# Pairwise Strassen K and V: the attention sum first in each batch, and one product of the first K half moved behind the odd batch's scores

## The reference

```python
x = x + xattn(layernorm(x), ctx)      # q = x Wq + bq ; k, v = split(ctx Wkv + bkv); rotary on q and k
                                      # 16 heads of 32: softmax(q k^T * 64**-0.5, mask) v, then Wo, bo
x = x + attn(layernorm(x))            # causal self attention, 16 heads
x = x + ffn(layernorm(x))             # 8 experts, the 2 best by the gate, softmax of their logits
```

## Time and profile before

| | |
|---|---|
| median of 3 runs | 830.67 us (829.15 to 832.28) |
| the profiled execution | 831.04 us, of it the span of instructions 829.2 us |
| mean granted TensorE clock | 0.961 |
| TensorE, matmuls | 760.4 us busy, 92% |
| VectorE | 574.8 us busy, 69% |
| ScalarE | 408.2 us busy, 49% |
| GpSimd | 340.0 us busy, 41% |

### The profile page before, as it was taken

The page is one execution under the profiler, slowest core; times in us unless marked ns, Lnnn a source line. Parts: engine busy times, 40 slices in busy tenths (PEclk is TensorE's granted clock), DMA queues, the critical chain, the costliest instruction groups (busy, mean ns, idle before and its releaser), DMA issues. The chain is left out here.

```text
span 829.2 us, 23209 instructions
## 1 busy us (share of the span) xinstructions
PE 760.4 (92%) x9494; PEld 660.5 (80%) x9495; DVE 574.8 (69%) x1293; ACT 408.2 (49%) x930; POOL 340.0 (41%) x364
## 2 busy tenths in 40 slices
PE   8999979979997997999899799798889999789997
PEld 7998869878896986888798688787667777668884
DVE  6766876975876686597577668746679998932236
ACT  5435646553563554555455464535447666213330
POOL 1654445454443644436354354522123222036740
PEclk9999999998999998999899999999999999969999
DMA  8211201111011010110101011013483234834548
GB/s 289 112 53 40 73 5 49 60 64 53 16 47 52 9 53 1 54 59 2 53 8 54 19 35 60 2 52 120 145 349 154 115 140 174 319 123 165 189 140 304
DMA packets 23317, 78.99 MB, mean 95 GB/s; under 512 B 3344, under 2 KB 4752, under 8 KB 20144
## 3 DMA queue, kind: packets, MB, share of 16 engines
q1 hardware_dynamic: 19536, 65.50, 21.7%
q0 software_dynamic: 3680, 12.06, 4.3%
HBM read 58.93 MB, written 18.61 MB: 94 GB/s over the span
## 5 line engine op out<-in xcount | busy, mean ns | idle before, releaser
L167 PE MATMUL quad<-wparts,othi 128*128 128x512 f32 (+1 forms) x104 | 49.2, 473 | 33.1 <-DVE otlo L1019 33.1
L501 POOL TENSOR_TENSOR wraw<-craw 128x516 f32<-128x516 f32 x14 | 18.6, 1326 | 135.9 <-issue 131.0
L1356 PE MATMUL bank<-ctx_parts_hi,wparts 128*128 128x258 f32 x224 | 68.7, 307 | 0.8 <-DVE ctx_parts_lo L890 0.7
L890 DVE TENSOR_TENSOR ctx_parts_lo<-craw,ctx_parts_hi 128x1032 fp32r<-128x1032 f32 (+1 forms) x56 | 64.8, 1158 | 2.6 <-ACT ctx_parts_hi L626 2.6
L1381 PE MATMUL bank<-wparts,ctx_parts_hi 128*128 128x256 f32 x224 | 64.6, 288 | 0.3 <-DVE kb_even L962 0.3
L1357 PE MATMUL bank<-ctx_parts_hi,wparts 128*128 128x258 f32 x224 | 63.5, 283 | 0.0
L1358 PE MATMUL bank<-ctx_parts_lo,wparts 128*128 128x258 f32 x224 | 63.4, 283 | 0.0
L1383 PE MATMUL bank<-wparts,ctx_parts_hi 128*128 128x256 f32 x224 | 63.0, 281 | 0.0
L1384 PE MATMUL bank<-wparts,ctx_parts_lo 128*128 128x256 f32 x224 | 62.8, 280 | 0.0
L626 ACT ACTIVATE ctx_parts_hi<-craw 128x1032 fp32r<-128x1032 f32 (+1 forms) x56 | 47.2, 843 | 26.9 <-POOL craw L509 26.6
L661 ACT ACTIVATE wraw<-wraw,nmax 128x257 f32<-128x257 f32 x96 | 47.9, 501 | 23.9 <-DVE nmax L983 23.9
(11 more groups left out here) (413 smaller groups left out, 2719.4 us busy)
## 6 DMA issues: line engine op xcount, KB each, us to landing
craw<-ctx_t_dram SPq DMA_DIRECT2D x32, 516.0 KB, 4.3
expert_lo<-weights_dram SPq DMA_DIRECT2D x8, 1024.0 KB, 12.2
expert_hi_scratch<-wraw SPq DMA_DIRECT2D x16, 512.0 KB, 2.6
wparts<-expert_hi_scratch SPq DMA_DIRECT2D x8, 1024.0 KB, 8.6
wraw<-weights_dram SPq DMA_DIRECT2D x6, 1024.0 KB, 4.9
expert_lo<-ffn_out_scratch SPq DMA_DIRECT2D x16, 256.0 KB, 5.2
x<-x_dram SPq DMA_DIRECT2D x8, 256.0 KB, 4.5
craw<-weights_dram SPq DMA_DIRECT2D x2, 1024.0 KB, 4.9
```

The lines of the kernel that those rows point to most:

```text
L167: pe.matmul(psum, ahi(c), bhi(c), start=(c == 0), stop=False)
L890: dve.tensor_tensor(dst[1], src, dst[0].bitcast(F32), ALU.subtract).then_inc(s_clo, 1)
L1356: pe.matmul(psum, whi_i[:, i, cols], hi[:, i, :], start=own and i == 0, stop=False, skip_group_check=not own)
```

## The change

It alters the order of the work and nothing of what is computed. On VectorE `o_sum(b - 1)` becomes the first work of each even and odd batch, `v_sum(p, S_11)` goes ahead of the masks of an even batch, and `o_lo` comes right behind the masks (even) or behind `pair_parts` (odd). ScalarE and GpSimd get `o_hi` and `o_bias` earlier to match; GpSimd does `diagonals` ahead of the context sums in an odd batch and behind them in an even one. TensorE does product (0, 6) of a pair behind the scores of the odd batch, where it stood at the end of the even one; ScalarE's `k_copy(q, 0, 6)` moves behind `exp(b, 0)` of the odd batch. In the odd batch the extra step, the spread diagonals and `attend` go ahead of (1, 7), and V's product 5 goes ahead of its product 2, so that `v_copy(p, 5)` moves into the odd batch. (1, 1) and (1, 3) change places, and the mask of the next batch is made later. In batch 3 `PLAIN - 1` is written as `PAIR_FIRST * 2 - 1`, the same number.

```diff
--- before.py
+++ after.py
@@ -306,10 +306,10 @@
             L_HI, L_LO, L_PRODUCT, L_COPY, L_SUM = range(1, 6)
 
 
-            K_PRODUCTS = ((0, 2), (0, 5), (0, 1), (0, 6), (0, 3), (0, 7), (1, 2), (1, 5), (0, 4), (1, 3), (1, 1), (1, 6),
+            K_PRODUCTS = ((0, 2), (0, 5), (0, 1), (0, 6), (0, 3), (0, 7), (1, 2), (1, 5), (0, 4), (1, 1), (1, 3), (1, 6),
                           (1, 7), (1, 4))
             K_COPIES = ((0, 5), (0, 1), (0, 6), (1, 5), (0, 4), (1, 1), (1, 6), (1, 4))
-            V_PRODUCTS = (2, 5, 1, 6, 3, 7, 4)
+            V_PRODUCTS = (5, 2, 1, 6, 3, 7, 4)
             V_COPIES = (5, 1, 6, 4)
 
             def k_product_of(q, c, k):
@@ -570,24 +570,24 @@
                         if b == PLAIN - 2:
                             ctx_sums_late(q)
                     elif b % 2 == 1:
+                        o_bias(b - 1)
+                        diagonals(b)
+                        if b < B - 1:
+                            k_sin(b + 1, 0)
                         if q <= PAIR_LAST:
                             ctx_sums_early(q)
-                        o_bias(b - 1)
-                        if b < B - 1:
-                            k_sin(b + 1, 0)
-                        diagonals(b)
                         if b < B - 1:
                             k_sin(b + 1, 1)
                         ln_and_bias(t, j)
                         if b < B - 1:
                             k_sin(b + 1, 2)
                     else:
+                        o_bias(b - 1)
                         for i in range(3):
                             k_sin(b + 1, i)
-                        o_bias(b - 1)
-                        diagonals(b)
                         if q <= PAIR_LAST:
                             ctx_sums_late(q)
+                        diagonals(b)
                         ln_and_bias(t, j)
                 ln_pool(pool, TILES + 1)
                 o_bias(B - 1)
@@ -784,16 +784,15 @@
                         k_copy(q, 0, 5)
                         part_hi(q, O_T4)
                         k_copy(q, 0, 1)
-                        k_copy(q, 0, 6)
 
                 def even_step(b, t, j):
                     p, q = b // 2, b // 2 + 1
                     more = q <= PAIR_LAST
                     last = t == TILES - 1
-                    v_copy(p, 5)
                     v_copy(p, 1)
                     if more:
                         part_hi(q, O_X1)
+                    before_o_hi(b)
                     exp(b, 0)
                     exp(b, 1)
                     v_copy(p, 6)
@@ -805,42 +804,42 @@
                     for g in range(G):
                         pt_evac(b, g)
                     v_copy(p, 4)
-                    before_o_hi(b)
                     if more:
                         part_hi(q, O_T32)
                         k_copy(q, 0, 5)
+                        k_copy(q, 0, 1)
                         part_hi(q, O_T4)
-                        k_copy(q, 0, 1)
                     if j == 0:
                         ln_apply(t + 1, x[:, 0 if last else t + 1, :])
-                    if more:
-                        k_copy(q, 0, 6)
-                    else:
+                    if not more:
                         w_hi(AK)
 
                 def odd_step(b, t, j):
                     p, q = (b + 1) // 2, (b + 3) // 2
                     last = t == TILES - 1
-                    for g in range(G):
+                    exp(b, 0)
+                    k_copy(p, 0, 6)
+                    for g in range(1, G):
                         exp(b, g)
                     k_copy(p, 1, 5)
+                    before_o_hi(b)
+                    k_copy(p, 0, 4)
                     pt_evac(b, 0)
                     pt_evac(b, 1)
-                    k_copy(p, 0, 4)
+                    k_copy(p, 1, 1)
                     pt_evac(b, 2)
                     pt_evac(b, 3)
-                    k_copy(p, 1, 1)
-                    next_mask(b)
-                    before_o_hi(b)
+                    k_copy(p, 1, 6)
                     if j == 1:
                         xt_hi(t + 1)
-                    k_copy(p, 1, 6)
                     if j == 3:
                         qt_evac(t + 1)
+                    next_mask(b)
                     if q <= PAIR_LAST:
                         part_hi(q, O_T1)
+                    v_copy(p, 5)
                     k_copy(p, 1, 4)
-                    if b == PLAIN - 1:
+                    if b == PAIR_FIRST * 2 - 1:
                         w_hi(WO)
                     if last:
                         act.wait_ge(s_qmm, TILES)
@@ -1136,13 +1135,14 @@
                     p, q = b // 2, b // 2 + 1
                     more = q <= PAIR_LAST
                     last = t == TILES - 1
+                    o_sum(b - 1)
+                    v_sum(p, S_11)
                     begin_step(b, j)
-                    v_sum(p, S_11)
+                    o_lo(b - 1, (b - 1) % BT)
                     if more:
                         part_lo(q, O_X1)
                     v_sum(p, S_12)
                     v_sum(p, S_22)
-                    o_sum(b - 1)
                     inverse_sums(b)
                     pair_parts(b)
                     if more:
@@ -1153,7 +1153,6 @@
                         if t == 2:
                             dve.wait_ge(s_x, 16 * (TILES - 1))
                         ln_stats(t + 1, x[:, 0 if last else t + 1, :])
-                    o_lo(b - 1, (b - 1) % BT)
                     if more:
                         part_lo(q, O_T32)
                     if j == 0:
@@ -1171,21 +1170,21 @@
                 def odd_step(b, t, j):
                     p, q = (b + 1) // 2, (b + 3) // 2
                     last = t == TILES - 1
+                    o_sum(b - 1)
                     begin_step(b, j)
                     k_sum(p, 0, S_12)
                     k_sum(p, 0, S_22)
                     if j == 3:
                         q_rotate(t + 1)
-                    o_sum(b - 1)
                     inverse_sums(b)
                     pair_parts(b)
+                    o_lo(b - 1, (b - 1) % BT)
                     k_cos(b + 1, 0)
                     k_sum(p, 1, S_11)
                     k_cos(b + 1, 1)
-                    o_lo(b - 1, (b - 1) % BT)
+                    k_sum(p, 1, S_12)
                     if j == 1:
                         xt_lo(t + 1)
-                    k_sum(p, 1, S_12)
                     k_sum(p, 1, S_22)
                     if q <= PAIR_LAST:
                         part_lo(q, O_T1)
@@ -1530,8 +1529,6 @@
                         k_product(PAIR_FIRST, 0, 1)
                     diagonals_spread(b)
                     attend(b, j)
-                    if b == PLAIN - 2:
-                        k_product(PAIR_FIRST, 0, 6)
 
                 def even_step(b, t, j):
                     p, q = b // 2, b // 2 + 1
@@ -1552,27 +1549,26 @@
                         k_product(q, 0, 1)
                     diagonals_spread(b)
                     attend(b, j)
-                    if more:
-                        k_product(q, 0, 6)
 
                 def odd_step(b, t, j):
                     p = (b + 1) // 2
+                    k_product(p, 0, 6)
                     k_product(p, 0, 3)
                     k_product(p, 0, 7)
                     k_product(p, 1, 2)
                     k_product(p, 1, 5)
+                    k_product(p, 0, 4)
                     probs_transposed(b)
-                    k_product(p, 0, 4)
+                    k_product(p, 1, 1)
                     k_product(p, 1, 3)
-                    k_product(p, 1, 1)
+                    k_product(p, 1, 6)
                     extra_step(b, t, j)
-                    k_product(p, 1, 6)
-                    v_product(p, 2)
+                    diagonals_spread(b)
+                    attend(b, j)
                     k_product(p, 1, 7)
                     v_product(p, 5)
                     k_product(p, 1, 4)
-                    diagonals_spread(b)
-                    attend(b, j)
+                    v_product(p, 2)
                     v_product(p, 1)
 
                 def last_step(b, j):
```

## The result

| | before | after |
|---|---|---|
| median | 830.71 us (829.15 to 832.28) | 785.83 us (784.58 to 787.63) |
| profiled execution, its span | 831.04, 829.2 us | 784.58, 782.8 us |
| mean granted TensorE clock | 0.961 | 0.984 |

The ratio is 0.946, with a 95% interval of 0.944 to 0.949 over four runs of each. The forecast was 792.0 (778 to 805): faster as said, and by 6 us more.

A forecast was written before the change was run, and what follows sets the result against it. TensorE sets the pace, its idle time is the gain, and VectorE's late masks limit it: seven pairs at 32.3 and six at 32.5 us save 39.7, batch 3 costs 1.0, giving 792.0 us (778 to 805).

The forecast's parts named there:

- The 45 us: Output product in seven even batches: the waits for `otlo` and the half clock behind them go, 45 us in all.
- The new wait: Ahead of (0,7) in the odd batch: TensorE waits 1.1 us for mask, exp and ScalarE's copy of the bank.
- a hole in VectorE's late stretch that waits for ScalarE: VectorE from `v_sum(S_22)` to the first odd mask: listed as a sign that the forecast is wrong; no size given.
- the 2.23 us of the earlier trace: Three `k_cos` at the stage's end: taken as their time alone, against 4.00 us beside the context sums.
- So 0.2 less: Pairs of a tile's batches 0 and 1: statistics (1.01 us) stand in for `q_trig` (1.21), so 32.3 us a pair.
- the 0.35 us of contention: VectorE's part `O_T32`: the later diagonals now fall on it, +0.35 us, estimated between 0 and 0.46.
- I leave the other small holes in: TensorE from (0,7) to the next even scores: only one hole of 0.27 us goes, 14.37 becoming 14.1 us.
- the zero for the swap of (1,1) and (1,3): TensorE's reordered products: each finds its sum or copy a product earlier; zero, bounded by 0.3 us either way.
- The little that may be lost lie ahead of the new wait and are covered by it: GpSimd's later diagonals, there by +13.2 us where TensorE wants them at about +13.1: no cost to the pair.
- VectorE doesn't bind: Rival: milder contention, mask in time, no wait ahead of (0,7); 52 us gained, 778 us; chance 0.18.
- The clock falls: Rival: wait ahead of (0,7) grows to 2.7 us, half clock costs 1.67 more; 43 us lost, 835 us; chance 0.03.
- Below 1.94 us the trace shows no fall, so it is decided there: TensorE's clock behind a wait: 1.94 us left it at 1.00, 4.73 us brought it to 0.62.

The follow-up runs named there:

- e3: The kernel before with the attention sum moved alone (GpSimd's diagonals as in the changed kernel, TensorE's product order kept); 779.78 us.
- e5: The changed kernel with GpSimd's diagonals back ahead of the late context sums in even batches; 790.14 us.
- e8: The changed kernel with GpSimd's two late context sums done on only 32 of 258 columns; 782.16 us.
- e1: The changed kernel with product (0,6) and its copy back at the end of the even batch; 779.28 us.
- e7: The changed kernel with the copy of (0,6) behind all four exps of the odd batch; 815.17 us.

## Why the prediction was right, and where it was off

**The 45 us were right.** All seven waits for `otlo` are gone, the clock in the stage is 1.00, and e3 shows that this part alone does it.

**The new wait was right in mechanism.** In the pair 2/3: mask +16.99 (forecast +16.91), (0,7) at +18.56 (+18.4), wait 0.80 us instead of 1.1 (0.96 if counted from the start that the forecast counted from, since TensorE was ready at +17.60, not at +17.29), and none where "issue" had taken it. The pair came out at 32.45 us on average against 32.5. But the sum that led there was right by luck, through two errors of opposite sign. It kept `k_cos` at 4.00 us, and it is 3.58, as the diagonals no longer lie beside its first part (e5, where they do: 3.98). And it said that VectorE would have no hole from `v_sum(S_22)` to the mask; it has one of 0.36, because the copy of (0,1) comes from TensorE, which hadn't become faster there. e8 shows that this is the binding link: with 2.2 us more slack on VectorE the mask doesn't move. The signpost "a hole in VectorE's late stretch that waits for ScalarE" was named as a sign against the forecast, and it is one. The second half of the pair was lucky too: (0,7) starts 0.16 us later than forecast, and the rest of the pair takes 13.87 us instead of 14.1.

The forecast also misread `k_cos`: it took the 2.23 us of the earlier trace rows for its time alone. GpSimd does its diagonals beside it there, in the kernel before:

```profile
570.20 0.62 POOL L533 TENSOR_TENSOR pdiag_hi<-p_last_and_rinv_hi,const 128x256 fp32r<-128x256 f32 x1
570.77 1.07 POOL L536 TENSOR_TENSOR pdiag_lo<-p_last_and_rinv_lo,const 128x256 fp32r<-128x256 f32 x1
```

With the sums on 32 columns (e8) it is 1.62. The sum didn't use this figure, but what VectorE pays for the sharing is larger than the forecast took it to be.

**The pair 0/1 is nearly the whole error of the sum.** Forecast 32.3, measured 31.29 on average (30.81 typically). 7 x 1.01 is 7.1 us of the 7.4 by which the stage (413.73) is under the forecast (421.1). Two terms of its sum were mis-sized:
- The mask was to stand at +16.7 and stands at +15.80; (0,7) starts at +17.37 instead of +18.2, with no wait listed. The forecast took the list of the pair 2/3 and exchanged two durations ("So 0.2 less"). It should have asked what GpSimd does beside each of them, and where in the list each stands. In the pair 0/1 the diagonals fall on the layernorm statistics, not on `O_T32`: the 0.35 us of contention in the sum are absent (1.22 against 1.64), `k_cos` is 0.42 shorter, and the inverse sums take 0.55 instead of 0.71 (237.44 to 237.99). There is no hole: the statistics stand ahead of `k_sum`, so the list reaches it at +14.01 (244.84), when the copy of (0,1) has ended, at +13.76. And from there to the mask it is 1.79 us, where the pair 2/3, with `q_trig` behind `k_sum`, has 3.12.
- From (0,7) to the next even scores the forecast had 14.1, 14.37 less one hole of 0.27. It is 13.44 here (261.64 - 248.20) and 13.87 in the pair 2/3. "I leave the other small holes in" was the step that failed, and with it the zero for the swap of (1,1) and (1,3). In the batch that was measured there was a second hole, 0.13 us ahead of V's product 5 (275.00 after 274.75), and a third ahead of (1,6), which waited for the copy of (1,1), the product right before it in the old order. Behind the four transposes of the extra step the next matmul, (1,6), came 0.74 us after their start; now it is the diagonals' matmul, after 0.36. First the kernel before, then the changed one:

```profile
270.81 0.60 PE L1233 MATMUL quad<-const,xn 128*128 128x128 f32 x4
271.55 0.39 PE L1356 MATMUL bank<-ctx_parts_hi,w_sums_hi 128*128 128x258 f32 x1
```

```profile
254.30 0.60 PE L1232 MATMUL quad<-const,xn 128*128 128x128 f32 x4
254.66 0.36 PE L1432 MATMUL quad<-pdiag_hi,same_head 128*128 128x256 f32 x1
```

In e3, which keeps the old order of products, it is 0.74 still. 0.27 + 0.13 + 0.38 is 0.78 of the 0.93 us; each broken place also cost 0.10 us on the matmul behind the break (last section), which about fills the rest.

**Against that, two costs weren't in the sum.** The even attention of the pair 2/3 waits 0.19 us for the diagonals, which run beside `O_T32`. e5, with the diagonals early, has its scores at +14.12 where the changed kernel has +14.59, so the late diagonals cost TensorE 0.47 us there; this doesn't show in the time, since (0,7) waits for the mask anyway. And the waits on "issue" (0.18, 1.06 and 0.96 us) fall into three pairs that are 0.3, 0.2 and 1.5 us longer than their like; the middle one only took the place of the wait ahead of (0,7). With the first pair, 32.41 us, which waits 1.10 us for a copy of V and 0.28 for the residual sum, they are why the pairs 0/1 are 31.29 on average and 30.81 typically. The forecast's "The little that may be lost lie ahead of the new wait and are covered by it" held in the pair 2/3.

**Small terms.** Batch 4 began 1.18 us later (forecast +1.0). The diagonals did take their cost from `O_22` (1.06 before, 332.84 - 332.23 = 0.61 after) to `O_T32`. The Trainium skill (GPSIMD Engine Reference, its table of specifications) speaks of VectorE operations with two SBUF inputs; the trace agrees here, since `BATCH_NORM_STATS2`, with one input, takes 0.68 us beside the diagonals (242.10) and 0.68 without them. Held against both kinds of pair ahead of the run, it would have pointed to the pair 0/1 as the one without that cost.

**The rivals.** "VectorE doesn't bind" (778) is the time of the kernel without the moved (0,6), e1 and e3. To go by the busiest engine, as this rival does, misses the wait in the changed kernel: there VectorE is busy 77% of the pair 2/3 and still sets it, through an order. "The clock falls" (835) is real in mechanism: the fall came after waits of 2.3 us (e7) and, outside the stage, of 1.74 (e1), less than the 2.7 in the forecast's case, and costs 1.46 us a time instead of 1.67 (e7). "Below 1.94 us the trace shows no fall, so it is decided there" doesn't hold across these runs. Behind its waits of 0.8 us the changed kernel's clock stayed at 1.00.

## What to carry to other kernels

When one change moves two things, price each alone: here the attention sum was worth 49 us, and the product moved with it cost 6 to 9 us that the total hid. When an instruction is moved behind another on an in-order engine, follow what that one waits for: the copy was cheap, but behind an exp it inherited the end of VectorE's list. And an estimate for one kind of batch isn't carried to another by exchanging durations; ask for each which other engine's work lies beside it, and where it stands in its queue.
